# Message passing on one core: where the three terms of an edge's message are added, and in which order the engines take their steps

## The reference, cut to what matters

```
x = x + _L1_gnn_ref(_layernorm(x, axis=-1), edge_index, edge_attr_64, L1_gnn_W1, L1_gnn_b1, L1_gnn_W2, L1_gnn_b2, ...)
```

## Time and profile before

| | |
|---|---|
| median of 3 runs | 7794.26 us (7785.04 to 7800.03) |
| the profiled execution | 7782.6 us, span 7780.9 us |
| mean granted TensorE clock over the span | 0.748 |
| the message pass, first gather to last sum | 3094.3 to 3789.6 us of the span |
| busy over the span | PE 64%, DVE 51%, ACT 30%, POOL 44% |

### The profile page before, as it was taken

One profiled execution on the slowest core, in us unless ns is written; L12 is line 12 of the kernel. 1 busy time (PEld: TensorE's weight loads), 2 busy tenths in 40 slices (PEclk: granted clock), 3 DMA queues, 4 the chain that ended last, 5 costly groups with the idle time before them and its releaser, 6 DMA issues. The chain is left out here.

```text
span 7780.9 us, 82688 instructions
## 1 busy us (share of the span) xinstructions
PE 4943.0 (64%) x21442; PEld 3404.9 (44%) x21443; DVE 3982.2 (51%) x11544; ACT 2332.1 (30%) x4547; POOL 3440.1 (44%) x3181
## 2 busy tenths in 40 slices
PE   1214966777772886667777467655996555455685
PEld 1103644555552554444554355544664323232474
DVE  8200025777777445677452577784435334343544
ACT  0002334554550112233212355543332222221122
POOL 4773015666662341777203455520003773676043
PEclk6555558988895897888885677777997767776687
DMA  2102432333332434555213222210002332333323
GB/s 46 28 21 69 137 110 80 97 96 95 94 92 65 129 114 62 161 161 164 76 39 86 75 69 71 68 35 14 17 8 70 93 92 60 93 92 92 103 79 103
DMA packets 377709, 633.66 MB, mean 81 GB/s; under 512 B 130352, under 2 KB 258451, under 8 KB 376033
## 3 DMA queue, kind: packets, MB, share of 16 engines
q0 software_dynamic: 146096, 360.51, 16.3%
q1 hardware_dynamic: 231005, 263.55, 12.9%
q10 hardware_dynamic: 308, 6.40, 0.3%
HBM read 474.19 MB, written 155.98 MB: 81 GB/s over the span
## 5 line engine op out<-in xcount | busy, mean ns | idle before, releaser
L784 POOL DMA_INDIRECT conv_rows<-rows_b,index x832 | 849.3, 1021 | 1228.6 <-SPq L2706 882.0
L816 DVE TENSOR_TENSOR acc<-acc,ps 125x257 f32 (+1 forms) x1664 | 701.1, 421 | 923.8 <-DMA acc<-slots,ffn_slot_of 379.8
L2752 PE MATMUL ps<-conv_rows,conv_weight_of 128*125 128x256 f32 x1664 | 624.9, 514 | 605.6 <-issue 269.7
L784 POOL DMA_INDIRECT gat_rows<-rows,index x416 | 558.6, 1343 | 818.8 <-POOLq L93 466.9
L2752 PEld LDWEIGHTS ps<-conv_rows,conv_weight_of 128*125 128x125 f32 x1664 | 359.7, 244 | 870.8 <-issue 538.3
L532 PE MATMUL ps<-front_L_gnn_W_t,front_attr_t 64*125 64x256 f32 x800 | 377.0, 648 | 419.3 <-issue 380.1
L784 POOL DMA_INDIRECT mpnn_rows<-rows_b,index x416 | 478.0, 1149 | 334.2 <-POOLq L1648 151.0
L333 POOL DMA_INDIRECT records_src<-by_src_edge_stage,by_src_edge_slot x400 | 410.1, 1025 | 449.2 <-DMA by_src_edge_stage<-edge_rows 177.9
L784 POOL DMA_INDIRECT hyp_rows<-rows,index x416 | 422.0, 1014 | 399.1 <-PE ps L2359 265.5
L2740 ACT ACTIVATE conv_weight_of<-conv_onehot_b,index 128x125 f32<-128x125 bf16 x832 | 251.5, 386 | 987.5 <-DVE conv_onehot_b L2724 754.4
L499 POOL DMA_INDIRECT records_dst<-front_back,front_dst_addr x400 | 417.4, 1044 | 214.4 <-issue 129.7
(11 more groups left out here) (591 smaller groups left out, 10529.6 us busy)
## 6 DMA issues: line engine op xcount, KB each, us to landing
mpnn_edge<-records_src SPq DMA_DIRECT2D x104, 512.0 KB
edge_rows<-front_edge_ring SPq DMA_DIRECT2D x100, 451.5 KB
by_src_edge_stage<-edge_rows SPq DMA_DIRECT2D x100, 451.5 KB
conv_rows<-rows_b,index POOLq DMA_INDIRECT x832
front_attr<-in_edge_attr SPq DMA_DIRECT2D x100, 112.0 KB
rows_b<-acc SPq DMA_DIRECT2D x15, 560.0 KB
second_w<-in_L_ffn_w SPq DMA_DIRECT2D x1, 8192.0 KB
slots<-mlp_y SPq DMA_DIRECT2D x56, 128.0 KB
```

The lines of the kernel that those rows point to most:

```text
L784: pool.indirect_dma_start(out=rows[:, n % U, t, :], out_offset=None, in_=table, in_offset=bass.IndirectOffsetOnAxis(ap=ends[:, n * G + t:n ...
L816: dve.tensor_tensor(here, here, S.ps[0:P, t % banks, 0:width], ALU.add).then_inc(added, 1)
L2752: pe.matmul(S.ps[0:P, t, 0:D], weight_of[:, q.slot, t, :], rows[:, q.slot, t, :], start=True, stop=True).then_inc(summed, 1)
```

## The change

Three things are changed in the message pass.

First, `message` adds the edge rows onto the bank instead of the bank onto the edge rows, so its result stays in the bank. `join` then adds two banks onto two tiles of gathered rows; there are four joins of two tiles a group where there were two of four. Second, the waits follow: a product waits for the join that read its bank, SP's next load of a half waits for the messages that read the half, and `joined` counts four a group. Third, DVE and PE have another written order, and `select` and the turning of one-hots stand in the middle of the round.

```
-                            sp.wait_ge(joined, 2 * q.n - 1 + half)
+                            sp.wait_ge(messages, (q.n - 1) * G + (half + 1) * (G // 2))
...
-                        v = edge[:, half, m, :]
-                        dve.tensor_tensor(v, v, S.ps[:, 2 + t % PB, 0:D], ALU.add).then_inc(messages, 1)
+                        v = S.ps[:, 2 + t % PB, 0:D]
+                        dve.tensor_tensor(v, v, edge[:, half, m, :], ALU.add).then_inc(messages, 1)
...
-                        at = slice(half * (G // 2), (half + 1) * (G // 2))
-                        dve.wait_ge(messages, q.n * G + at.stop)
-                        v = rows[:, q.slot, at, 0:D]
-                        dve.tensor_tensor(v, v, edge[:, half], ALU.add).then_inc(joined, 1)
+                        dve.wait_ge(messages, q.n * G + 2 * m + 2)
+                        v, bank = rows[:, q.slot, 2 * m:2 * m + 2, 0:D], 2 + 2 * m % PB
+                        dve.tensor_tensor(v, v, S.ps[:, bank:bank + 2, 0:D], ALU.add).then_inc(joined, 1)
...
+                pipeline(dve, (2, message(0)), (2, message(1)), (2, join(0)), (2, message(2)), (2, message(3)),
+                         (3, add_up(0)), (2, join(1)), (3, add_up(1)), (0, select), (2, message(4)),
+                         (2, message(5)), (3, add_up(2)), (2, join(2)), (3, add_up(3)), (2, message(6)),
+                         (2, message(7)), (3, add_up(4)), (2, join(3)), (3, add_up(5)), (3, add_up(6)),
+                         (3, add_up(7)), written_out=True)
...
-                        act.wait_ge(joined, 2 * q.n + half + 1)
+                        act.wait_ge(joined, (q.n * 2 + half + 1) * 2)
...
-                            pe.wait_ge(messages, q.n * G + t - PB + 1)
+                            pe.wait_ge(joined, q.n * (G // 2) + (t - PB) // 2 + 1)
...
+                pipeline(pe, *products_of(0, 1, 2, 3), *sums_of(0, 1), (1, turn_one_hots), *products_of(4, 5),
+                         *sums_of(2, 3), *products_of(6, 7), *sums_of(4, 5, 6, 7))
```

More of the change, by code:

```diff
@@ L1754, in stage, with join, add_up @@
                         dve.wait_ge(products, q.n * G + t + 1)
-                        v = edge[:, half, m, :]
-                        dve.tensor_tensor(v, v, S.ps[:, 2 + t % PB, 0:D], ALU.add).then_inc(messages, 1)
+                        v = S.ps[:, 2 + t % PB, 0:D]
+                        dve.tensor_tensor(v, v, edge[:, half, m, :], ALU.add).then_inc(messages, 1)
                     return stage
-                def join(half):
+                def join(m):
                     def stage(q):
-                        if half == 0:
+                        if m == 0:
                             dve.wait_ge(gathered[q.slot], rows_in(q))
-                        at = slice(half * (G // 2), (half + 1) * (G // 2))
-                        dve.wait_ge(messages, q.n * G + at.stop)
-                        v = rows[:, q.slot, at, 0:D]
-                        dve.tensor_tensor(v, v, edge[:, half], ALU.add).then_inc(joined, 1)
-                    return stage
[L1769 to L1774, removed]
+                        dve.wait_ge(messages, q.n * G + 2 * m + 2)
+                        v, bank = rows[:, q.slot, 2 * m:2 * m + 2, 0:D], 2 + 2 * m % PB
+                        dve.tensor_tensor(v, v, S.ps[:, bank:bank + 2, 0:D], ALU.add).then_inc(joined, 1)
+                    return stage
+                def add_up(t):
+                    return lambda q: accumulate(dve, S, q, ids, D + 1, 2, summed, added, [t])
+                pipeline(dve, (2, message(0)), (2, message(1)), (2, join(0)), (2, message(2)), (2, message(3)),
[3 more added lines that the diff above has]
+                         (3, add_up(7)), written_out=True)
             @block.scalar
@@ L1836, in _, with products_of, sums_of @@
                 pe.wait_ge(ready, 2)
-                pipeline(pe, (1, turn_one_hots), *(
-                    stage for t in range(G) for stage in ((2, product_of(t)), (3, sum_of(t)))))
+                def products_of(*tiles):
+                    return [(2, product_of(t)) for t in tiles]
+                def sums_of(*tiles):
+                    return [(3, sum_of(t)) for t in tiles]
+                pipeline(pe, *products_of(0, 1, 2, 3), *sums_of(0, 1), (1, turn_one_hots), *products_of(4, 5),
+                         *sums_of(2, 3), *products_of(6, 7), *sums_of(4, 5, 6, 7))
         gru(nc, S, A)
```

## The result

| | before | after |
|---|---|---|
| median of 3 runs, us | 7794.26 | 7870.35 (7858.72 to 7887.59) |
| profiled execution, us | 7782.6 | 7870.35 |
| first joins, first to last group, / 51 | 13.12 us | 14.77 us |

What follows compares the result with a forecast made beforehand. Waits set the pace before; after, DVE at 10.7 and POOL at 10.8 us would mesh at 11.1 a round against 13.12, saving 103 us over 51 rounds: 7690 us, range 7645 to 7745 (forecast itself 7670 to 7712).

Steps and rivals of the forecast that it cites:

- the one-hots without a wait: DVE, mid-round: one-hots no longer wait for ACT's widening, taking away all of 2.04 us a round.
- the relu wait on PE: PE, relu to sum: products run during the relu, so the wait falls from 126.7 to under 30 us.
- rival 3: DVE messages: writing into the bank costs x more each; from x = 0.30 us the pass is slower; chance 0.05.
- the join at 0.68: DVE joins of 512 columns: trace duration 0.69 us, counted as 0.61 each, 2.44 a round for four.
- the gather at 1.00: POOL gathers: average falls to near 1.04 us from 1.16, as joins no longer have both operands in SBUF.
- the 9.6: DVE's own work a round: messages 2.76, joins 2.44, accumulations 3.27, one-hots 1.11; 0.9 us more than before.
- the forecast 11.1: Message pass: us a round, as DVE and POOL with four slots between them won't mesh fully; before 13.12.
- POOL's 10.8: POOL's round: 8 x 1.26 + 0.73 us, only the one-hots still stretching one gather.
- DVE's 10.7: DVE's round in us: own work, plus remote waits 0.5 and half of the waits for PE, 0.6.
- the forecast gain: Message pass: 51 x (13.12 - 11.1) = 103 us saved.
- Rival 2: PE's clock binds, every second round slow: period about 12.0 us, 57 us saved, 7737 us; chance 0.14.
- The share of 0.05 for slower: Whole kernel: chance given to a run slower by more than about 0.2%, 16 us.

Runs made afterwards that it cites:

- the data path alone: Changed kernel with DVE's and PE's lists in the old order; ratio to before 1.0034 on a chip with late PE updates, 0.9953 with prompt ones.
- the path with moved one-hots: Changed kernel with PE's and DVE's old order, only DVE's one-hots moved mid-round; ratio to before 1.0086 on a chip with late PE updates.
- the order alone: Changed kernel with messages and joins back in SBUF; ratio to before 1.0054 on a chip with late PE updates, 0.9951 with prompt ones.

## Why the prediction was wrong

- Right: the one-hots without a wait, the relu wait on PE from 126.7 to 0.7, the message at 0.43 us with the bank as its target (0.41 before, so rival 3's price x was 0.01 and not 0.30), the join at 0.68, the gather at 1.00. POOL has slack on kind L only; on kind P it is the bound, with DVE close behind (10.20 us without gathers).
- Wrong: the step "To the 9.6 I add the remote waits as they are, 0.5, and half of the waits for PE, 0.6". I took the 1.1 us as a fixed price. On kind L the term measured 4.8, and 9.6 + 4.8 is 14.4 of the 14.77. On kind P it measured 0.7, with 0.7 more for gathered rows (33.3 us). What the runs show in its place: on kind L these waits are in the main PE's updates landing late while gathers run, since without gathers a round takes 10.2 us there. Before, 176 of the 190 late updates belong to the last three products and sums of a round, the turning and the next round's first product, where PE and DVE stood still for relu and widening anyway. After, 281 of the 378 belong to the turning, the last four products and sums 2 and 3, with DVE's and ACT's work right behind them. That the filled pause is what doubled them is only argued, and can't be all: with PE's old order the data path alone (249 of 708 late) and the path with moved one-hots (307 of 735) lose too.
- Wrong at its base as well: the 13.12 us of before had two causes, the wait for the widening and the lateness. On kind P the period before was 11.62, so there even the 10.76 of after saves 51 x 0.86 = 44 us and not 103. That the 10.76 lies near the forecast 11.1 is in part luck: POOL's 10.8 held (10.6 measured), but DVE's 10.7 had waits in it that were read off late updates. No version that does all the work had the forecast gain on either kind.
- The rivals: the price of the bank write was the only one on the slower side, and the loss came another way. Rival 2 saw a low clock, for another reason: the clock fell (0.85 to 0.74), and ahead of each of its 38 falls in the changed pass PE had stood still for over 1 us. The share of 0.05 for slower was far too small for a trace with waits that I couldn't explain.
- Two slips in the sums bear on nothing: by their own prices the accumulations are 2 x 0.63 + 6 x 0.33 = 3.24 us, not 3.27, and a period of 10.6 us gives 7666, not 7670.
- What I had and didn't use: among the waits of before, 3100 to 3795 us, stands one of ACT that I left out of the earlier trace rows. On kind P ACT has no such wait:

```profile
ACT mpnn_rows L1789 <- issue: 138.2, 29, 9.5
```

The trace of before also shows PE starved beside POOL's indirect transfers in another place, where they write rows out instead of gathering them. A stretch of the front layer, before on kind L, then the same on kind P:

```profile
300.00:400.00 100.00, 14.24 (x36) 8.97 (x36) 0.00 (x0) 5.52 (x12) 76.06 (x79) 0.50 0.09 21
```

```profile
300.00:400.00 100.00, 100.00 (x259) 64.04 (x258) 0.00 (x0) 39.33 (x86) 75.91 (x80) 1.00 0.51 138
```

PE's group there, 250 to 600 us, before on kind L and on kind P:

```profile
L532 PE MATMUL ps<-front_L_gnn_W_t,front_attr_t 64*125 64x256 f32 x88 | 41.5, 647 | 313.9 <-issue 313.9
```

```profile
L532 PE MATMUL ps<-front_L_gnn_W_t,front_attr_t 64*125 64x256 f32 x600 | 283.0, 651 | 0.0
```

POOL issues at the same rate (79 and 80), and PE does a seventh of the work while waiting for nothing that the profile shows. The clock isn't the cause: in the run without gathers on kind L, which leaves the front layer as it is, this stretch has a granted clock of 1.00 and the same 14.24 us of PE.

## What to carry to other kernels

Count a "remote" or "issue" wait that no engine explains as a resource of its own, find where it recurs, and ask what the change puts behind it; don't carry its old total over. A wait that is taken off one engine is only won if the engine behind it has other work to run, as the one-hots moved alone show. And a gain of 1% may have the other sign on another chip of the same type: compare only on one chip, and look at a second.

## What the hardware showed that I had not expected

- On some chips PE's semaphore updates land up to 22 us after the matmul while POOL's gathers run, and promptly without them; on others never over 0.1 us. The whole kernel took 7844 us on one of the first and 6919 on one of the second. How much of this the late updates cost isn't shown. Between the traces of before on kind L and kind P, 864 us apart, the first join of the message pass comes 612 us later on kind L, so most lies ahead of the pass, and of that only the front layer was looked at.
- The cause within the chip stays open. In the traces of kind L many semaphore events are missing as well, and not of PE alone. Of the 6656 steps by which the pass's 416 gathers report that they have landed, the traces of before and after hold 3213 and 1763 on kind L, and 6619 and 6592 on kind P. Of PE's 884 updates they hold 718 and 811 on kind L, and 884 and 870 on kind P. This points to the recording of the trace. The Trainium skill, "NOTIFIC — the notification-queue block", section "Overflow: three behaviours, one of which stalls the engine", says that the block that writes trace records holds its producers back rather than lose a record inside, so that the recording can slow an engine. That would fit the late updates, though not by itself the missing events; no run here was made without the recording, so it isn't shown, and how much faster the kernel would be without it is open.
- A VectorE addition with its target in a bank takes 428 ns on average where one with its target in SBUF takes 415. The gathers shorten from 1149 to 998 ns with the joins' second operand in a bank: on kind P the data path alone gives 1011, the order alone 1075, the kernel before 1101.
